# The third attention of a two-block transformer kernel: maxima in two halves of the heads, and another order of slots

## The reference, cut to what matters

```python
xn = _ln(x, lnx_g, lnx_b)
yn = _ln(y, lny_g, lny_b)
q = jnp.einsum('bsc,hcd->bhsd', xn, wq)
k = jnp.einsum('btc,hcd->bhtd', yn, wk)
v = jnp.einsum('btc,hcd->bhtd', yn, wv)
a = jax.nn.softmax(jnp.einsum('bhsd,bhtd->bhst', q, k) * D ** (-0.5), axis=-1)
o = jnp.einsum('bhst,bhtd->bhsd', a, v)
o = o.transpose(0, 2, 1, 3).reshape(x.shape[0], x.shape[1], H * D)
x_out = x + o @ li1_w + li1_b
```

## Time and profile before

| | us |
|---|---|
| median of 3 runs | 1419.69 (1417.68 to 1422.72) |
| the profiled execution | 1417.98 |
| its span in the trace | 1416.3 |
| TensorE busy (matmul) | 1294.0, 91% |
| VectorE busy | 979.2, 69% |
| ScalarE busy | 850.2, 60% |
| GpSimd busy | 662.6, 47% |

### The profile page before, as it was taken

One profiled execution on the slowest core, in us unless ns is written; L12 is line 12 of the kernel. 1 busy time (PEld: TensorE's weight loads), 2 busy tenths in 40 slices (PEclk: granted clock), 3 DMA queues, 4 the chain that ended last, 5 costly groups with the idle time before them and its releaser, 6 DMA issues.

```text
span 1416.3 us, 41562 instructions
## 1 busy us (share of the span) xinstructions
PE 1294.0 (91%) x17195; PEld 836.7 (59%) x17214; DVE 979.2 (69%) x2222; ACT 850.2 (60%) x1365; POOL 662.6 (47%) x1134
## 2 busy tenths in 40 slices
PE   7899999998999998899999999988987888899995
PEld 3455555554455554456777777665755555677585
DVE  6688888875565555677888888764577887876243
ACT  3677777775666665657777777654465656532352
POOL 4455555543000002245766766453347776454265
PEclk8999999997999999999999999999999999998898
DMA  7000000000410000000000000002001111132451
GB/s 226 3 3 3 3 2 3 3 3 2 121 51 1 1 0 1 1 1 18 33 21 29 33 25 26 32 32 61 1 26 46 47 46 47 39 99 79 132 168 46
DMA packets 55181, 53.70 MB, mean 38 GB/s; under 512 B 9305, under 2 KB 49245, under 8 KB 54738
## 3 DMA queue, kind: packets, MB, share of 16 engines
q1 hardware_dynamic: 51090, 44.20, 10.1%
q0 software_dynamic: 2816, 6.11, 1.2%
q10 hardware_dynamic: 1088, 0.72, 0.3%
HBM read 20.34 MB, written 14.49 MB: 25 GB/s over the span
## 4 chain that ended last, share of the span: by engine, by line
PE 67%; DVE 11%; POOL 7%; issue 4%; ACT 4%; DMA 3%; SPq 3%; POOLq 0%; ACTq 0%; DVEq 0%
PE psum L1561 6%; PE psum L1589 4%; PE psum L949 4%; PE psum L1223 4%; PE psum L950 4%; PE psum L951 4%; PE psum L1187 3%; PE psum L2615 3%; DVE c_nm L2108 2%; SPq L803 2%; DMA a_QT<-a_nmT 2%; PE psum L529 2%; DVE c_rden L2136 2%; DVE a_nm L611 2%; PE psum L1532 2%
## 5 line engine op out<-in xcount | busy, mean ns | idle before, releaser
L1644 DVE TENSOR_REDUCE b_nm<-psum 128x4 f16<-128x1024 f32 x128 | 156.6, 1223 | 52.0 <-PE psum L1566 51.4
L728 ACT ACTIVATE a_prob<-psum 128x768 f32<-128x768 f32 (+1 forms) x160 | 136.1, 853 | 63.8 <-PE psum L466 62.1
L611 DVE TENSOR_REDUCE a_nm<-psum 128x4 f16<-128x1024 f32 (+1 forms) x96 | 117.3, 1223 | 43.9 <-PE psum L496 30.9
L780 POOL TENSOR_SCALAR_AFFINE_SELECT a_prob<-a_prob 128x512 f32<-128x512 f32 x128 | 81.8, 639 | 126.6 <-ACT a_prob L728 126.3
L171 POOL TENSOR_TENSOR f_ln_rstd<-f_ln_tmp,pow_half 128x4 f32<-128x4 f32 x24 | 25.4, 1058 | 200.0 <-DVE f_ln_tmp L160 200.0
L1077 ACT ACTIVATE xo_sb<-psum,f_w_h_s 128x512 f32<-128x512 f32 x64 | 44.0, 688 | 88.3 <-PE psum L951 88.3
L1561 PE MATMUL psum<-b_QTh,b_KTh 32*128 32x256 f16 x512 | 70.4, 272 | 6.9 <-DVE b_nm L1644 5.2
L1566 PE MATMUL psum<-b_KTh,b_QTh 32*128 32x256 f16 x512 | 70.8, 273 | 0.0
L1566 PE MATMUL psum<-b_KTh,b_QTl 32*128 32x256 f16 x512 | 69.6, 269 | 0.0
L1566 PE MATMUL psum<-b_KTl,b_QTh 32*128 32x256 f16 x512 | 69.6, 269 | 0.0
L1561 PE MATMUL psum<-b_QTh,b_KTl 32*128 32x256 f16 x512 | 69.3, 268 | 0.0
(11 more groups left out here) (454 smaller groups left out, 4536.0 us busy)
## 6 DMA issues: line engine op xcount, KB each, us to landing
f_h_wh<-b_rden SPq DMA_DIRECT2D x64, 128.0 KB, 2.1
f_h_wh<-c_rden SPq DMA_DIRECT2D x64, 128.0 KB
expert_in<-empty SPq DMA_DIRECT2D x8, 662.5 KB, 10.3
m_xt<-expert_in SPq DMA_DIRECT2D x7, 662.5 KB, 5.7
m_w<-in_L_ffn_w_dram SPq DMA_DIRECT2D x16, 256.0 KB, 2.6
x_sb<-in_x_dram SPq DMA_DIRECT2D x8, 256.0 KB, 4.8
f_w_h_w<-in_L_ffn_h_w_dram SPq DMA_DIRECT2D x2, 1024.0 KB, 7.4
out_dram<-m_send SPq DMA_DIRECT2D x8, 256.0 KB, 2.8
```

The lines of the kernel that those rows point to most:

```text
L611: nc.vector.tensor_reduce(out, psum[:, banks, :].rearrange("p i (a b) -> p i a b", a=groups), X, ALU.max, negate=True).then_inc(max_done, 1)
L728: nc.scalar.activation(prob[unit % 5][:, :, 0:width], psum[:, first:first + 2, 0:width], ACT.Exp, scale=SCALE).then_inc(exp_done, 1)
L780: nc.gpsimd.affine_select(out=diagonal, in_=diagonal, compare_op=ALU.is_ge, fill=0.0, base=0, pattern=[[0, 4], [1, P]], channel_multiplier ...
L1644: v.tensor_reduce(self.nm[:, :, :].rearrange("p t (j r) -> p j t r", r=32)[:, 2 * e:2 * e + 2, :, g], self.pr.psum[:, 2:4, :].rearrange("p ...
```

## The change

The maxima are made and reduced in two halves of the heads: strips 0 and 1 (banks 0 and 1) and strips 2 and 3 (banks 2 and 3), each over all 256 queries. The first half waits for the first exponential of the batch before, the second for the second. They wait for the high copies, no longer for the low ones; the scores wait for the low ones instead. All parts have other slots, on every engine; in each slot that is 1 modulo 8 the projections stand ahead of the scores on TensorE and ScalarE.

```diff
--- before.py
+++ after.py
@@ -1849,9 +1849,10 @@
 
 
     U, G, D = 8, 4, 32
-    SLOT = {"z": -11, "k": -8, "q0": -7, "q1": -6, "v": -4, "nm": -1, "o": 14}
-    SCORES, VALUES, MAXIMA = {0: 0, 1: 2}, {0: 3, 1: 5}, -4
-    FIRST, LAST = -23, 8 * (B - 1) + 17
+    SLOT = {"v": -6, "z": -14, "nm": -2, "k": -10, "q0": -9, "q1": -7, "o": 12}
+    SCORES, VALUES, MAXIMA = {0: 0, 1: 1}, {0: 3, 1: 5}, {0: -5, 1: -4}
+    LOWS = {"k": -9, "q0": -8, "q1": -7}
+    FIRST, LAST = -28, 8 * (B - 1) + 15
 
     tail, steps, tail_vector, tail_gpsimd = 8 * B - 2, 8 * B - 1, 8 * B - 11, 8 * B - 9
     NORMS = {8 * B - 11: [(0, 0)], 8 * B - 9: [(0, 1)], 8 * B - 8: [(1, 0)], 8 * B - 4: [(1, 1)]}
@@ -1995,19 +1996,18 @@
                                     start=(i == 0 and g == 0), stop=(g == self.G - 1), skip_group_check=True)
         inst.then_inc(self.pro_full, 1)
 
-    def tensor_max(self, n):
+    def tensor_max(self, n, half):
 
         t, D, G = self.nc.tensor, self.D, self.G
-        self.tensor_drained(("k", n))
         if n:
-            t.wait_ge(self.exp_done, 2 * n)
-        else:
+            t.wait_ge(self.exp_done, 2 * n - 1 + half)
+        elif half == 0:
             t.wait_ge(self.banks_free, self.banks_free_at)
+        if half == 0:
+            t.wait_ge(self.high, self.highs[("q1", n)])
         for g in range(G):
-            if g % 2 == 0:
-                self.tensor_drained((f"q{g // 2}", n))
             for i in range(2):
-                for j in range(4):
+                for j in (2 * half, 2 * half + 1):
                     q, to = slice(D * j, D * j + D), (i * G + g) * TC
                     inst = t.matmul(self.pr.psum[:, j, to:to + TC], self.QT[n % 2][0][q, g, i * P:i * P + P],
                                     self.KT[n % 2][0][q, g, :], start=(g + i == 0), stop=True, skip_group_check=True)
@@ -2015,8 +2015,10 @@
 
     def tensor_scores(self, n, e):
         t, D = self.nc.tensor, self.D
+        t.wait_ge(self.max_done, 2 * n + e + 1)
         if e == 0:
-            t.wait_ge(self.max_done, 2 * (n + 1))
+            self.tensor_drained(("k", n))
+        self.tensor_drained((f"q{e}", n))
         to = lambda i, j: self.pr.psum[TC * (j % 2):TC * (j % 2) + TC, 2 * e + j // 2, i * T:i * T + T]
         for i in range(2):
             for (x, y) in ((0, 0), (0, 1), (1, 0)):
@@ -2066,14 +2068,19 @@
         inst.then_inc(self.av_done, 1)
 
     def tensor_slot(self, s):
+        ahead = s % self.U == 1
+        if ahead:
+            for use in self.parts(s, self.SLOT):
+                self.tensor_projection(use)
         for e, n in self.parts(s, self.SCORES):
             self.tensor_scores(n, e)
-        for _, n in self.parts(s, {0: self.MAXIMA}):
-            self.tensor_max(n)
+        for half, n in self.parts(s, self.MAXIMA):
+            self.tensor_max(n, half)
         for e, n in self.parts(s, self.VALUES):
             self.tensor_values(n, e)
-        for use in self.parts(s, self.SLOT):
-            self.tensor_projection(use)
+        if not ahead:
+            for use in self.parts(s, self.SLOT):
+                self.tensor_projection(use)
 
 
     def vector_normed(self, n, k):
@@ -2099,15 +2106,14 @@
             self.ln_c.vector_normalise(n, self.zc[n % 2], ctx).then_inc(self.z_ready, 1)
             self.ln_x.vector_normalise(n, self.z[n % 2], un).then_inc(self.z_ready, 1)
 
-    def vector_max(self, n):
-        v = self.nc.vector
-        v.wait_ge(self.max_full, n + 1)
-        if n:
+    def vector_max(self, n, half):
+        v, pair = self.nc.vector, slice(2 * half, 2 * half + 2)
+        v.wait_ge(self.max_full, 2 * n + half + 1)
+        if n and half == 0:
             v.wait_ge(self.pro_full, self.ring.full(("nm", n - 1)))
-        for i in range(2):
-            v.tensor_reduce(self.nm[:, i, :].rearrange("p (j r) -> p j r", r=32)[:, :, 0:self.G],
-                            self.pr.psum[:, 0:4, i * T:i * T + T].rearrange("p j (g k) -> p j g k", g=self.G), X, ALU.max,
-                            negate=True).then_inc(self.max_done, 1)
+        v.tensor_reduce(self.nm[:, :, :].rearrange("p t (j r) -> p j t r", r=32)[:, pair, :, 0:self.G],
+                        self.pr.psum[:, pair, :].rearrange("p j (t g k) -> p j t g k", t=2, g=self.G), X, ALU.max,
+                        negate=True).then_inc(self.max_done, 1)
 
     def vector_low(self, use):
 
@@ -2144,19 +2150,20 @@
         v.tensor_tensor(self.oT[:, :, :], self.num[n % 2][:, :, :], self.rb[:, :, :], ALU.mult).then_inc(self.oT_ready, 1)
 
     def vector_slot(self, s):
-        for _, n in self.parts(s, {0: self.MAXIMA}):
-            self.vector_max(n)
-        for use in self.parts(s, self.SLOT):
-            if use[0][0] in "qk":
-                self.vector_low(use)
-        for _, n in self.parts(s, {0: 6}):
+        for half, n in self.parts(s, self.MAXIMA):
+            self.vector_max(n, half)
+        for k, n in self.parts(s, {3: -23}):
+            self.vector_normed(n, k)
+        for _, n in self.parts(s, {0: 7}):
             self.vector_rden(n)
-        for _, n in self.parts(s, {0: 11}):
+        for use in self.parts(s, self.LOWS):
+            self.vector_low(use)
+        for _, n in self.parts(s, {0: 10}):
             self.vector_scaled(n)
-        if s == self.U * (B - 1) + 15:
+        if s == self.U * (B - 1) + 14:
             self.nc.vector.wait_ge(self.x_done, B - 1)
             self.output(self.nc.vector, B - 1)
-        for k, n in self.parts(s, {4: -13, 0: -23, 1: -21, 2: -18, 3: -16}):
+        for k, n in self.parts(s, {0: -28, 4: -19, 1: -26, 2: -26}):
             self.vector_normed(n, k)
 
 
@@ -2204,11 +2211,16 @@
         a.activation(self.num[n % 2][:, 2 * e, :], self.pr.psum[:, 4, 0:T], ACT.Copy).then_inc(self.num_out, 1)
 
     def scalar_slot(self, s):
+        ahead = s % self.U == 1
+        if ahead:
+            for use in self.parts(s, self.SLOT):
+                self.scalar_projection(use)
         for e, n in self.parts(s, self.SCORES):
             self.scalar_scores(n, e)
-        for use in self.parts(s, self.SLOT):
-            self.scalar_projection(use)
-        for e, n in self.parts(s, {0: 3, 1: 5}):
+        if not ahead:
+            for use in self.parts(s, self.SLOT):
+                self.scalar_projection(use)
+        for e, n in self.parts(s, self.VALUES):
             self.scalar_values(n, e)
 
 
@@ -2241,17 +2253,17 @@
         g.tensor_tensor(x, x, self.more[:, :, :], ALU.add).then_inc(self.x_done, 1)
 
     def gpsimd_slot(self, s):
-        for _, n in self.parts(s, {0: -11}):
+        for _, n in self.parts(s, {0: -13}):
             self.gpsimd_low(n)
+        for _, n in self.parts(s, {0: -27}):
+            self.ln_in.gpsimd_rstd(n)
+        for _, n in self.parts(s, {0: -25}):
+            self.gpsimd_unnormed(n)
+        for _, n in self.parts(s, {0: -24}):
+            self.ln_c.gpsimd_rstd(n)
         for _, n in self.parts(s, {0: -22}):
-            self.ln_in.gpsimd_rstd(n)
-        for _, n in self.parts(s, {0: -20}):
-            self.gpsimd_unnormed(n)
-        for _, n in self.parts(s, {0: -17}):
-            self.ln_c.gpsimd_rstd(n)
-        for _, n in self.parts(s, {0: -15}):
             self.ln_x.gpsimd_rstd(n)
-        for _, n in self.parts(s, {0: 16}):
+        for _, n in self.parts(s, {0: 14}):
             self.gpsimd_output(n)
 
 
```

## The result

The changed kernel takes 1441.65 us (median of 4 runs, 1439.79 to 1445.20), beside 1420.78 us of the kernel before on the same chip (4 runs, 1417.68 to 1422.72): a ratio of 1.0152, with a 95% interval of 1.0122 to 1.0182. Its profiled execution took 1440.12 us, with a span of 1438.4; before it was 1417.98 and 1416.3.

What follows compares the result with a forecast made beforehand. Bound: VectorE's ring of scaling, work up to the reciprocal, DMA, scaling. Terms -0.4 + 11.6 + 0.8 + 4.3 = 16.3 us on the profiled 1417.98 gave 1434 us; own range 1424 to 1440, whole range 1416 to 1443.

Steps and rivals of the forecast that it cites:

- The ring named: Third attention: VectorE from scaling to reciprocal, DMAs, next scaling set the period; 6.74 + 4.77 = 11.51 us before, 12.7 after.
- VectorE's run to the reciprocal: VectorE's work from the scaling's start to the reciprocal's end: 8.04 us after the change against 6.74 before.
- the DMA leg: Reciprocal's end to the next scaling, over four DMAs: 4.65 us taken as mean, ends 4.04 and 5.19, untouched by the change.
- The signs named: Trace after: scalings 12.1 to 13.2 us apart, reciprocal's end 8.0 us behind scaling, TensorE waiting before o, o(14) before last values.
- rival 3: Third attention heavier than summed: long leg, dearer low copies, maxima or TensorE clock; 13.2 us periods, 1441 us and above; chance 0.08.
- head: Start of the third attention: first scaling 0.4 us earlier, between -2 and +2.
- 13 periods: First waiting scaling to batch 13's scaling: 13 x 12.69 = 165.0 us against 153.4, so +11.6.
- scaling 13 to 14: Near the stage's end, no input norms left: reciprocal at +5.84, DMA 4.65, 12.25 us against 11.5, so +0.8.
- tail: Stage's end: last values, transposes with ScalarE's pass, and first hidden product come behind o(14); 4.2 us, say +4.3.
- The halves and TensorE: Two-strip products on TensorE: up to 0.45 us more a batch, hidden in the wait before o; maxima's reductions priced unchanged.
- Rival 2: TensorE is the bound, its waits for maxima and low copies the price; 10.3 us periods, 1402 us; chance 0.15.
- Rival 1: DMA leg no longer decides (under 3.4 us or hidden); GpSimd's chain sets 11.45 us periods, 1417.3 us; chance 0.11.

Runs made afterwards that it cites:

- two_dma: Changed kernel with two of the four DMAs of each batch's reciprocals left out from batch 1 on, output partly not computed: 1424.57 us, ratio 1.003.
- send_after: Changed kernel with all four DMAs kept, two of each batch's issued by ScalarE instead of SP: 1447.01 us, ratio 1.012.
- output15: Changed kernel with GpSimd's output part one slot later, 15 for 14, behind the un-normalising: 1439.05 us, ratio 1.0138.
- warm: Changed kernel with 6 and 20 products that nobody reads on TensorE ahead of o(13) and o(14): 1456.69 us, ratio 1.0179.
- halves_only: Kernel before the change with its maxima in two halves of the heads and no slot moved: 1431.05 us beside 1430.83, ratio 0.9998.
- stats_early: Changed kernel with the input statistics two slots earlier, ahead of VectorE's scaling and so beside the DMAs: 1452.25 us, ratio 1.0171.
- scale12: Changed kernel with VectorE's scaling two slots later, 12 for 10, behind both maxima: 1487.43 us, ratio 1.0486.
- warm_all15: Changed kernel with GpSimd's output at slot 15 and unread products ahead of every o (4, 6 at batch 13, 20 at 14): 1443.51 us, ratio 1.0098.

## Why the prediction was right

**The mechanism held; two of its sizes did not, and partly by luck.** The ring named (VectorE's run to the reciprocal plus the DMA leg) closes in the trace after to the hundredth, and two_dma and send_after moved the quick periods by what they took off the leg. The signs named came: scalings 12.90 to 12.92 us apart in seven of the 13 periods, TensorE waiting for the scaling ahead of o and no longer for the maxima, o(14) ahead of the last values. One did not: the reciprocal's end is 8.86 us behind the scaling's start and not 8.0. The forecast of 1434 us was 7.6 short of 1441.65. That is inside the whole range (1416 to 1443) by 1.4 us, but outside the forecast's own (1424 to 1440), in the field of rival 3, to which I had given 0.08. As a ratio the forecast was 1.0115, and 1.0152 was measured (1.0122 to 1.0182). By its steps, against the profiled execution:

| step | predicted | measured | what was mis-sized |
|---|---|---|---|
| head | -0.4 | -0.1 | |
| 13 periods | +11.6 | +15.8 | run 8.04, was 8.86 in most (mean 8.77); leg 4.65, was 4.03 to 4.06 in most (mean 4.24) |
| scaling 13 to 14 | +0.8 | +1.9 | slow o, late reciprocal |
| tail | +4.3 | +4.5 | |
| sum | +16.3 | +22.1 | |

**The run.** The price of the input's normalisation was the term that was mis-sized. I took 0.52 us for it from before, where no addition of GpSimd ran beside it. In the new order GpSimd's additions start at 1122.41, as the timeline says (the second instruction of the pair is shown by itself):

```profile
1121.72 0.72 POOL L171 TENSOR_TENSOR c_lni_rstd<-c_lni_tmp,pow_half 128x2 f32<-128x2 f32 x1
1122.41 0.73 POOL L2133 TENSOR_TENSOR xo_sb<-c_res,c_w_li_b 128x256 f32<-128x256 f32 x1
1123.14 0.88 DVE L188 TENSOR_SCALAR c_zi<-u_sb,c_lni_mv,c_lni_rstd 128x128 f32<-128x128 f32 x1
1123.22 0.72 POOL L2135 TENSOR_TENSOR xo_sb<-xo_sb,u_sb 128x256 f32<-128x256 f32 x1
...
1126.06 2.48 SPq L2277 DMA_DIRECT2D f_h_wh<-c_rden  x4
```

and the pair of normalisations at 1122.55 takes 1.47 us. The first of the pair ends at 1123.22 and the second at 1124.02, each 0.08 us behind the end of the addition beside it (1123.14 and 1123.94), as if each had stood until that addition was over. output15 moved those additions and the 0.87 went. The sum had priced GpSimd's work as a queue and not as something that makes VectorE's instructions longer.

**The leg.** 4.03 to 4.06 us behind most reciprocals is the short end of what I had read the earlier trace rows, not the mean; here SP's four issues took 2.48 us (1126.06). In the three periods in which the leg was 4.83 to 5.05 us (scalings at 1065.55, 1156.68 and 1184.97) the issues took 3.07, 3.17 and 3.42. The DMA view of the first 3 us behind a reciprocal's end says what comes with it; for the leg of 5.05 us (1179.92 to 1182.92) it has this line:

```profile
q8 instruction: 1, 0.02, 2.7%
```

These are the queue and its kind, its packets, MB and its share of the 16 engines: one 16 KB transfer of the instruction queue starts in these 3 us. The same view has one behind each of the four legs of 4.32 to 5.05 us and behind none of the other twelve (4.03 to 4.10 us). In the kernel before, nine of the ten legs of 4.57 to 5.18 us have one, and none of the five of 4.04 to 4.17 us has (the last scaling, 7.06 us behind its reciprocal, did not wait for the DMA; with it four of the sixteen did not, where I had counted three). In two_dma the legs of 3.87, 4.00, 4.45 and 4.55 us have one, though SP's two issues took 1.17 us each time, so there it is the transfers that came late. So the mean of 4.65 was a mix of legs with and without such a load, and the changed kernel met fewer of them. That is what goes together in the traces; no run moved the loads by themselves.

So the 0.59 that the leg gave back and the 0.82 that the run cost nearly cancel in the quiet periods: 12.92, predicted 12.69. This is luck: 13 periods with the run as it was and my leg of 4.65 would have been 5.3 us longer, and the total about 1447 us, outside the range of 1416 to 1443.

**The long periods.** The seven steady ones alone would give 13 x 12.91 - 153.4 = +14.4; the four long ones add 4.0 and the two short ones take 2.7 back. Three of the four are long by their leg alone (4.83, 4.83 and 5.05 us). The fourth, 14.38, is long through o: at 1156.68 the leg had been 4.83 us, o then started at 1158.05 after 1.81 us of idle time and took 3.76 us, and the reciprocal behind it (1165.26) waited 1.79 us for ScalarE's copies. I had left 0.4 us between that chain and VectorE, worked out with an o of 1.95 us. At the stage's end it is the same: behind o(13) the reciprocal started at 1228.29, 7.25 us after the scaling where I had 5.84, and its leg was 4.32 for 4.65; 1.41 less 0.33 is the 1.1 that the step from 13 to 14 missed. In warm, with o(13) at 2.05 us, that step was 11.52 and not 13.33. So the clock is not what makes most long periods in this trace. After the long legs of 1065.55 and 1184.97, with 1.80 and 2.03 us of idle time ahead of them, o took its 2.02 us and the next period was 12.90.

**The halves and TensorE.** Priced at nothing on the path, and halves_only agrees (0.9998). Rival 2 (TensorE's waits were the price) is out: they did go, and the kernel got slower. The Trainium skill ("TensorEngine Tiling (Array Packing)", section "Key Properties") has tiles on different strips working in parallel; halves on two strips took 12.8 us where four strips took 9.4, so 1.36 times and not twice: the trace agrees in direction, and none of it is on the path. Rival 1 needed a leg under 3.4 us, with the run as I had it; with the run of 8.86 it is under 2.6. send_after, at 3.25, still had 12.12, and two_dma, at 2.75, 11.61 with 0.23 us of waiting left: near that chain, and still on the DMA's side. Rival 3 had the right size (1441 and above) and half of its reasons: not a leg at its long end, but TensorE's clock, with 1.5 us in the period of 14.38 and 1.1 in the step from 13 to 14. What it did not name, the dearer normalisation, was the larger part.

**The tail.** +4.5 for +4.3 predicted, but not shown piece by piece: the slow o(14) (1.6 us over 2.02) is in it and was not in the sum, so that the two agree is in part luck, and the order alone was not run by itself.

## What to carry to other kernels

In a loop in which each engine works in a fixed order, add up the rings (one engine's run from the consumer of a transfer to its producer, plus the transfer's leg) and compare the sum with the period; a move that ends the largest wait of the busiest engine is worth nothing when it puts work into the run ahead of the transfer. Price a moved instruction with what will run beside it, not with its duration where it stood. A leg read from a trace can be a mix of two lengths; look for what goes with the long ones before taking the mean. Before moving the end of a ring, walk the next two rings through the new order: here the first repairs of one ran into a ring through the projections, one through o and its copies, and one through GpSimd.

## What the runs showed of the hardware

- Two normalisations on VectorE (128x128, float32, both in the on-chip memory) take 0.60 us alone and 1.47 us beside GpSimd additions of 128x256 float32, up to 1.68 in stats_early. GpSimd's additions stayed at 0.72 to 0.73. Where the scaling on VectorE had started first, it was GpSimd's instruction that took longer: in the kernel before, a small TENSOR_SCALAR (L168) took 1.20 us beside the scaling of 1074.48, and 0.22 without it.
- The 16 products of o take 2.02 us in quiet batches after, and 3.48 to 3.76 us at three places, where TensorE had stood for 1.55 to 4.93 us before them; with fillers ahead of them 2.05 us in all but one batch. The idle time just before does not decide it alone: o took 2.02 us after 1.80 and 2.03 us in the changed kernel, and 3.63 and 3.56 us after 1.03 us in output15 (1079.40 and 1130.52). The granted clock over 1060 to 1180 was 1.00 of the full level of 2.4 GHz before, 0.97 after, 0.83 in scale12, and 1.00 in warm_all15.
- Four DMA issues on SP took 2.46 to 2.48 us in most batches of the changed kernel, and 3.07 to 3.42 in three; the scaling that waits for the transfers started 4.03 to 4.06 and 4.83 to 5.05 us behind the reciprocal's end. Each of its legs of 4.32 us and more had a 16 KB transfer of the instruction queue that started within 3 us of the reciprocal's end, and no shorter one had.
